# One wide matmul for state and outputs, and the right sides moved to the front of the slot

## The reference

```
bS = einsum('bhk,bhkv->bhv', b_t, S)
S  = exp(g)[..., None] * S + a_t[..., None] * bS[:, :, None, :] + k_t[..., None] * v_t[:, :, None, :]
o  = einsum('bhk,bhkv->bhv', q_t, S)
```

## Time and profile before

| | |
|---|---|
| median of 3 runs | 2630.47 us (2616.48 to 2632.16) |
| span of the profiled execution, first to last instruction | 2622.0 us |
| PE / DVE / ACT / POOL busy | 87% / 61% / 62% / 17% |
| DMA | 338.90 MB, 129 GB/s mean, queue q1 busy 48.2% |
| granted PE clock, mean | 0.950 |

### The profile page before, as it was taken

The page is one execution under the profiler, slowest core; times in us unless marked ns, Lnnn a source line. Parts: engine busy times, 40 slices in busy tenths (PEclk is TensorE's granted clock), DMA queues, the critical chain, the costliest instruction groups (busy, mean ns, idle before and its releaser), DMA issues.

```text
span 2622.0 us, 225147 instructions
## 1 busy us (share of the span) xinstructions
PE 2288.4 (87%) x102472; PEld 1721.9 (66%) x102472; DVE 1601.7 (61%) x3940; ACT 1618.0 (62%) x3048; POOL 458.8 (17%) x555
## 2 busy tenths in 40 slices
PE   6788898999988899998999998989999988999785
PEld 2556666666666666666676666666666666766573
DVE  2456366666556676656666665666666566666533
ACT  3556466666666666656666666666666666666543
POOL 1011111111111111111111111111111111111210
PEclk7879899999999999999999999999999999999987
DMA  3244455534555554455554455555445555534541
GB/s 95 74 110 121 110 148 148 141 104 127 145 141 151 137 141 111 132 138 146 144 137 118 124 145 146 148 141 142 113 129 143 145 148 148 136 103 132 140 125 41
DMA packets 692934, 338.90 MB, mean 129 GB/s; under 512 B 551794, under 2 KB 651728, under 8 KB 692816
## 3 DMA queue, kind: packets, MB, share of 16 engines
q1 hardware_dynamic: 692816, 337.67, 48.2%
HBM read 35.57 MB, written 16.78 MB: 20 GB/s over the span
## 4 chain that ended last, share of the span: by engine, by line
PE 86%; issue 10%; DVE 2%; ACT 1%; DMA 1%; SPq 0%; ACTq 0%; DVEq 0%
PE bank L570 14%; PE bank L733 13%; PE bank L712 11%; PE bank L704 8%; PE bank L724 7%; PE bank L716 5%; PE bank L593 5%; PE bank L683 5%; PE bank L622 5%; PE bank L643 3%; PE bank L577 3%; PE bank L694 2%; PE bank L602 2%; PE bank L587 2%; PE bank L584 2%
## 5 line engine op out<-in xcount | busy, mean ns | idle before, releaser
L473 POOL TENSOR_TENSOR state<-moved,edge 128x512 f32<-128x512 f32 x252 | 292.3, 1160 | 1821.9 <-DVE moved L1093 1821.9
L712 PE MATMUL bank<-parts,w_now 32*32 32x64 f32 x16512 | 420.1, 223 | 4.8 <-DMA w_now<-w_row 3.6
L570 PE MATMUL bank<-x_col,w_kqv 128*128 128x512 f32 x768 | 370.6, 619 | 48.5 <-issue 47.9
L856 ACT ACTIVATE parts<-bank,cf 128x256 f32<-128x256 f32 x512 | 214.6, 470 | 319.5 <-DVE o_col L1087 310.7
L716 PE MATMUL bank<-aq_now,delta 32*32 32x16 f32 x16512 | 403.7, 179 | 9.2 <-issue 9.2
L716 PEld LDWEIGHTS bank<-aq_now,delta 32*32 32x32 f32 x16512 | 391.7, 110 | 6.7 <-issue 6.7
L712 PEld LDWEIGHTS bank<-parts,w_now 32*32 32x32 f32 x16512 | 377.2, 110 | 17.1 <-issue 5.0
L733 PE MATMUL bank<-uq_now,s_now 32*32 32x24 f32 x32768 | 362.2, 189 | 14.5 <-issue 14.4
L733 PEld LDWEIGHTS bank<-uq_now,s_now 32*32 32x32 f32 x32768 | 337.1, 107 | 24.1 <-issue 18.2
L1116 DVE COPY_PREDICATED aq<-ci,bank 128x128 f32<-128x128 int32 x256 | 77.1, 301 | 410.3 <-PE bank L704 276.7
L1087 DVE TENSOR_TENSOR o_col<-qs,bank 128x64 f32<-128x64 f32 x512 | 89.5, 216 | 388.6 <-PE bank L716 384.7
(11 more groups left out here) (99 smaller groups left out, 3814.1 us busy)
## 6 DMA issues: line engine op xcount, KB each, us to landing
s_now<-state SPq DMA_DIRECT2D x256, 256.0 KB
uq_now<-uqv SPq DMA_DIRECT2D x256, 192.0 KB
t_now<-t_t SPq DMA_DIRECT2D x256, 128.0 KB, 2.0
w_now<-w_row SPq DMA_DIRECT2D x256, 128.0 KB
uq_a<-uqv SPq DMA_DIRECT2D x64, 384.0 KB
low<-uqv SPq DMA_DIRECT2D x64, 384.0 KB
x_col<-in_xt_dram SPq DMA_DIRECT2D x32, 512.0 KB, 5.8
w_a<-w_col SPq DMA_DIRECT2D x64, 256.0 KB
```

What stands on the lines that cost most here:

```text
L473: pool.tensor_tensor(state[:, qc, :, :, :].rearrange("p m b v -> p (m b) v"), moved[m % 2][:, :, :, :].rearrange("p m b v -> p (m b) v"), ...
L570: mm = pe.matmul(ps[:, :], w_kqv[:, a, w, f * P:(f + 1) * P], x_col[:, a, :], start=a == 0, stop=a == KT - 1)
L712: pe.matmul(ds_bank[quarter(h), m, :, :].rearrange("p b v -> p (b v)"), w_now[quarter(h), m, :], parts[quarter(h), m, :, :].rearrange("p b ...
L856: act.activation(parts[:, :, b, :], p2_bank, ACT.Copy, scale=cf[:, C_TAKE + b:C_TAKE + b + 1])
```

## The change

`updates` becomes one matmul per tile and head, of 80 columns: `delta` is now the weights, and the moving side is `wa_now`, which holds the masked rows of w for sequence 0 (32 columns) and for sequence 1 (32 columns) and `aq` (16 columns). The change of the state comes out transposed. So:

- PE: `updates` is 32 matmuls of 80 columns in place of 32 of 64 and 32 of 16. A slot runs `right_sides`, `deltas`, `updates`, then the dense work. `right_sides` waits for `first_in` (the loads of `uq_now` and `s_now`) and for `qs_copied` of the slot before; `deltas` for `second_in` (`t_now` and the `aq` piece); `updates` for `w_masked`.
- SP: the load of `w_now` is gone. The order of issue in a slot stays `t_now`, `aq`, then `uq_now` and `s_now`.
- POOL: a new `mask_part` ahead of each `decay_part`, two one-input multiplications of 128x256 from `w_row` into `wa_now`. `decay_part` has a new addition state + change (128x512) ahead of the multiplication by the decay.
- DVE: L1093 is replaced by two transposes of 128x256 from PSUM into `change`.
- ACT: the two copies to `parts` are gone; the copy to `delta` stays.

```diff
+    PIECE = GB * TB
+    WIDE = GB * HD + PIECE
+    PIECES = WIDE // PIECE
...
-        w_now = sb("w_now", [P, CT, HD])
-        parts = sb("parts", [P, CT, GB, HD])
-        aq_now = sb("aq_now", [P, CT, GB * TB])
+        wa_now = sb("wa_now", [P, PIECES, CT, PIECE])
...
-        ds_bank = psum[2][:, :].rearrange("p (m b v) -> p m b v", m=CT, b=GB)
+        up_bank = wide[:, :, 0:QI * WIDE].rearrange("p f (q c) -> p f q c", c=WIDE)
+        p2_bank = wide[:, :, QI * WIDE:QI * (WIDE + HD)].rearrange("p f (q v) -> p f q v", v=HD)
...  (SP, behind p3_filled)
-                        sp.dma_start(aq_now[:, :, :],
-                                     chunk(aq[c if n >= 1 else 1 - c], m)).then_inc(aq_in.handle, 16)
-                        sp.dma_start(by_pairs(w_now[:, :, :]),
-                                     of_chunks(by_pairs(w_row[c if n >= 1 else 1 - c][:, :, :]),
-                                               m)).then_inc(w_in.handle, 16)
+                        sp.dma_start(wa_now[:, PIECES - 1, :, :],
+                                     chunk(aq[c if n >= 1 else 1 - c], m)).then_inc(second_in.handle, 16)
...  (POOL)
+            def mask_part(j, c, n):
...
+                rows = of_chunks(by_pairs(w_row[own][:, :, :]), m).rearrange("p q (f k e) -> p q f k e", f=HF, e=PIECE)
...
+                pool.wait_ge(p3_filled.handle, made)
+                for b in range(GB):
+                    dst = wa_now[:, 2 * b:2 * b + 2, :, :].rearrange("p k (q f) e -> p q f k e", f=HF)
+                    pool.tensor_scalar(dst, rows, cf[:, C_TAKE + b:C_TAKE + b + 1], None,
+                                       ALU.mult).then_inc(w_masked.handle, 1)
...  (POOL, decay_part)
+                mine = state[:, qc, :, :, :].rearrange("p m b v -> p (m b) v")
+                pool.wait_ge(s_turned.handle, s_turned.at(g, m + 1))
+                pool.tensor_tensor(mine, mine, change[m % 2][:, :, :, :].rearrange("p m b v -> p (m b) v"),
+                                   ALU.add).then_inc(s_added.handle, 1)
                 pool.wait_ge(s_added.handle, s_added.at(g, m + 1))
...
-                pool.tensor_tensor(state[:, qc, :, :, :].rearrange("p m b v -> p (m b) v"),
-                                   moved[m % 2][:, :, :, :].rearrange("p m b v -> p (m b) v"),
-                                   decay.unsqueeze(2).to_broadcast([P, CT * GB, HD]),
+                pool.tensor_tensor(mine, mine, decay.unsqueeze(2).to_broadcast([P, CT * GB, HD]),
                                    ALU.mult).then_inc(state_ready.handle, 1)
...  (PE, updates)
-                        pe.matmul(ds_bank[quarter(h), m, :, :].rearrange("p b v -> p (b v)"), w_now[quarter(h), m, :],
-                                  parts[quarter(h), m, :, :].rearrange("p b v -> p (b v)"),
-                                  start=True, stop=True)
-                    for h in range(HPH):
-                        mm = pe.matmul(o_bank[quarter(h), m, :], delta[quarter(h), m, :], aq_now[quarter(h), m, :],
-                                       start=True, stop=True)
+                        mm = pe.matmul(up_bank[quarter(h), m % HF, m // HF, :].rearrange("p (k e) -> p k e", e=PIECE),
+                                       delta[quarter(h), m, :], wa_now[quarter(h), :, m, :], start=True, stop=True)
...  (PE, slot)
-                pe.wait_ge(x_turned.handle, turn)
-                pe.wait_ge(t_in.handle, turn16)
-                pe.wait_ge(delta_ready.handle, turn)
-                pe.wait_ge(o_added.handle, turn)
-                deltas()
-
-                pe.wait_ge(set_up.handle, N_SET_UP)
-                pe.wait_ge(w_in.handle, turn16)
-                pe.wait_ge(aq_in.handle, turn16)
-                pe.wait_ge(s_added.handle, turn)
-                updates()
-
-                pe.wait_ge(set_up.handle, N_SET_UP)
-                pe.wait_ge(uq_in.handle, turn16)
-                pe.wait_ge(s_in.handle, turn16)
+                pe.wait_ge(first_in.handle, turn32)
                 pe.wait_ge(qs_copied.handle, turn)
                 right_sides()
+
+                pe.wait_ge(set_up.handle, N_SET_UP)
+                pe.wait_ge(second_in.handle, turn32)
+                deltas()
+
+                pe.wait_ge(set_up.handle, N_SET_UP)
+                pe.wait_ge(w_masked.handle, turn2)
+                updates()
...  (ACT, delta_part)
-                act.wait_ge(o_added.handle, o_added.at(j, n - 1))
-                for b in range(GB):
-                    act.activation(parts[:, :, b, :], p2_bank, ACT.Copy, scale=cf[:, C_TAKE + b:C_TAKE + b + 1])
-                act.activation(delta[:, :, :], p2_bank, ACT.Copy).then_inc(delta_ready.handle, 1)
+                act.wait_ge(s_turned.handle, s_turned.at(j, n - 1))
+                act.activation(delta[:, :, :].rearrange("p (q f) v -> p f q v", f=HF), p2_bank,
+                               ACT.Copy).then_inc(delta_ready.handle, 1)
...  (DVE, update)
-                dve.tensor_tensor(moved[m % 2][:, :, :, :], mine, ds_bank, ALU.add).then_inc(s_added.handle, 1)
+                dst = change[m % 2][:, :, :, :].rearrange("p (q f) b v -> p f q (b v)", f=HF)
+                for f in range(HF):
+                    last = dve.transpose(dst[:, f, :, :], up_bank[:, f, :, 0:GB * HD])
+                last.then_inc(s_turned.handle, 1)
```

More of the change, by code:

```diff
@@ L165, in delta_block @@
         t_now = sb("t_now", [P, CT, HD])
-        w_now = sb("w_now", [P, CT, HD])
-        parts = sb("parts", [P, CT, GB, HD])
-        aq_now = sb("aq_now", [P, CT, GB * TB])
+        wa_now = sb("wa_now", [P, PIECES, CT, PIECE])
         state = sb("state", [P, QC, CT, GB, HD])
-        moved = [sb(f"moved{c}", [P, CT, GB, HD]) for c in range(2)]
+        change = [sb(f"change{c}", [P, CT, GB, HD]) for c in range(2)]
         x_now = sb("x_now", [P, CT, HD])
@@ L196, in delta_block @@
         lora_b = y_col[0:UD, 0, D:2 * D]
-        psum = [ctx.enter_context(nc.psum_tensor(f"bank{i}", [P, BANK], F32)) for i in range(8)]
+        wide = ctx.enter_context(nc.psum_tensor("wide", [P, HF, BANK], F32))
+        single = [ctx.enter_context(nc.psum_tensor(f"bank{i}", [P, BANK], F32)) for i in range(6)]
+        psum = [single[0], wide[:, 0, :], wide[:, 1, :]] + single[1:]
         p1_bank = psum[0][:, 0:CT * GB * RQ].rearrange("p (m b r) -> p m b r", m=CT, b=GB)
-        p2_bank = psum[1][:, 0:CT * HD].rearrange("p (m v) -> p m v", m=CT)
-        o_bank = psum[1][:, CT * HD:CT * (HD + GB * TB)].rearrange("p (m r) -> p m r", m=CT)
-        ds_bank = psum[2][:, :].rearrange("p (m b v) -> p m b v", m=CT, b=GB)
+        up_bank = wide[:, :, 0:QI * WIDE].rearrange("p f (q c) -> p f q c", c=WIDE)
+        p2_bank = wide[:, :, QI * WIDE:QI * (WIDE + HD)].rearrange("p f (q v) -> p f q v", v=HD)
         a_banks = [psum[3 + i][:, 0:CT * GB * RQ].rearrange("p (m b r) -> p m b r", m=CT, b=GB) for i in range(PAIR)]
@@ L358, in stage_first @@
             def stage_first(c, n):
-                sp.dma_start(uq_now[:, :, :], of_chunks(uqv[c][:, :, 0:HF * UQ], n)).then_inc(uq_in.handle, 16)
-                sp.dma_start(s_now[:, :, :, :], state[:, n % QC, :, :, :]).then_inc(s_in.handle, 16)
+                sp.dma_start(uq_now[:, :, :], of_chunks(uqv[c][:, :, 0:HF * UQ], n)).then_inc(first_in.handle, 16)
+                sp.dma_start(s_now[:, :, :, :], state[:, n % QC, :, :, :]).then_inc(first_in.handle, 16)
             def iteration(j, c):
@@ L456, in _ @@
             pool.wait_ge(weights_in.handle, n_weights)
+            def mask_part(j, c, n):
+                if not (there(j) and not (isinstance(j, int) and j * CH + n == 0) or (there(j - 1) and n < 1)):
+                    return
+                g, m, own = (j, n - 1, c) if n >= 1 else (j - 1, CH - 1, 1 - c)
+                rows = of_chunks(by_pairs(w_row[own][:, :, :]), m).rearrange("p q (f k e) -> p q f k e", f=HF, e=PIECE)
+                if m == 0:
+                    pool.wait_ge(w_turned.handle, w_turned.at(g, 1))
+                made = held(pool, until, p3_filled.at(j, n + 1))
+                pool.wait_ge(set_up.handle, N_SET_UP)
+                pool.wait_ge(p3_filled.handle, made)
[3 more added lines that the diff above has]
+                                       ALU.mult).then_inc(w_masked.handle, 1)
             def decay_part(j, c, n):
@@ L723, in deltas @@
                     for h in range(HPH):
-                        mm = pe.matmul(p2_bank[quarter(h), m, :], t_now[quarter(h), m, :], x_now[quarter(h), m, :],
+                        mm = pe.matmul(p2_bank[quarter(h), m % HF, m // HF, :], t_now[quarter(h), m, :], x_now[quarter(h), m, :],
                                        start=True, stop=True)
```

56 lines of the change are left out of this document (28 added, 28 removed).

## The result

The changed kernel takes 2745.21 us (median of 4 runs, 2732.57 to 2755.27), the kernel before beside it 2631.31: a ratio of 1.0455 over all their runs, with a 95% interval of 1.0399 to 1.0511 (the two medians alone give 1.043). So it is 4.5% slower. Forecast were 2720 and a range of 2590 to 2790. The profiled execution is the fastest of the four, 2732.57, on a span of 2730.7.

What follows compares the result with a forecast made beforehand. PE bounds A; PE and DVE run neck and neck in B. A 41.0 + B 37.8 = 78.8 against 75.9 us, +2.9 times 31 groups = +90 on 2622, 2712; the median lies 8.5 higher: 2720, range 2590 to 2790.

Steps and rivals of the forecast that it cites:

- B: Stretch from the end of `updates` in slot 4 to slot 0's first scores: 34.6 us before, forecast 37.8.
- `updates` from 1.53 to 1.10 us: On PE, the 80-column matmuls shorten `updates` by 0.43 us per slot, with bounds of 0.35 and 0.83.
- A: Stretch from slot 0's first scores to the end of `updates` in slot 4: 41.3 us before, forecast 41.0, bound by PE.
- Loads hidden in slots 4 to 6, 0.9 us in slot 7: Later-issued `uq_now` and `s_now` hide behind the dense part by 0.6 us in slots 4 to 6; slot 7 stalls 0.9.
- U: The end of `updates` in a slot, from which load times are counted; `s` was forecast landed 3.7 us after it.
- DVE's four gaps in B go, -1.5 us: DVE's waits for PE in B (0.33, 0.23, 0.40, 0.54 us) vanish, since `right_sides` is done before DVE's update.
- Masks 0.45 each, at most 0.73: Time on POOL of each of the two new one-input products of 128x256: 0.45 us, upper end 0.73.
- Contention, 4.1 us in B: POOL's work delays DVE's two-SBUF-input instructions, 0.8 us per us: 2.2, 0.5, 0.95, 0.45 in slots 4 to 7.
- The signs: Expected in the trace: `updates` 1.1 us, POOL near 1,200 us, longer solve and L1246, B 37 to 38 us.
- Rival 3: On PE, the 80-column matmul is no shorter than both were: 2773 us; chance 0.1 together with dearer POOL work.
- rival 2: In B, half the contention, 2.05 us, making a group 76.75 us and the time 2657; chance 0.16.
- Rival 1: In DVE's solve and products in B, no contention worth naming: group 74.7 us, time 2593; chance 0.24.

Runs made afterwards that it cites:

- 5: The changed kernel with PE's order put back to deltas, updates, right sides: 2689.83 us, 1.0225 of the kernel before.
- 8: The changed kernel with masks on ACT, PE's old order and POOL's addition of state and change left out: 2579.14 us, 0.9827 of the kernel before.
- 4: The changed kernel with the loads of `uq_now` and `s_now` issued earlier, right behind `right_sides`: 2732.44 us, 1.0426 of the kernel before.
- 2: The kernel before with only PE's order changed to right sides, deltas, updates: 2810.70 us, ratio 1.0688.
- 9: The changed kernel, new order kept, with masks on ACT and without POOL's addition of state and change: 2574.67 us, 0.9802 of the kernel before.
- 10: The changed kernel without POOL's addition of state and change, masks still on POOL: 2583.45 us, 0.9845 of the kernel before.
- 3: The kernel before with PE's new order and the loads of `uq_now` and `s_now` issued first, right behind `right_sides`: 2683.81 us, ratio 1.0227.
- 1: The kernel before with four unused 128x256 instructions on POOL per slot, two one-input and two two-input: 2760.93 us, ratio 1.0517.
- 6: The changed kernel with the masks moved from POOL to ACT: 2673.26 us, 1.0177 of the kernel before.
- 11: The changed kernel with six unused 512-column matmuls per group, three before slot 0's first scores, three in slot 5: 2680.66 us, 1.0211 of the kernel before.
- 7: The changed kernel with masks on ACT and PE's order of the kernel before: 2628.32 us, 1.0009 of the kernel before.
- Experiment 12: The changed kernel with masks on ACT, PE's old order and two unused matmuls in slot 0: 2645.26 us, 1.0081 of the kernel before.

## Why the prediction was right

It was right in sign, in size (2720 against 2745) and in the mechanism (POOL's new work delays DVE, which sets B), but terms of both stretches were wrong and partly cancelled. Point by point:

- **`updates` from 1.53 to 1.10 us: right,** 1.10 in 5. That it pays when POOL gets no more work is shown by 8, with the addition left out: 1.7% at most.
- **A at 41.0 us: 39.5.** PE's busy time in A fell by 0.74 us, from 37.82 to 37.08, where +1.42 and four times -0.43 made -0.30, and its idle time fell from 3.5 to 2.4, which I had left as it was. Why was not tested.
- **Loads hidden in slots 4 to 6, 0.9 us in slot 7: right in effect, not in the steps.** `s_now` is issued 1.4 us behind `updates` (1444.18), as I had it, and takes 2.7 us to land (median), not 2.2, so it lands at U + 4.1 and not at U + 3.7. Slot 7 did not stall, because its dense part, with a wait of 1.34 us for L1275, was longer. In the whole span PE waits 39.8 us for `s_now`, in 18 waits, and taking them out (4) brings 0.3%. How near it was is shown by 2 (150.5 us, with the old load of w ahead) and by 9 and 10 (74 us, with PE less late by DVE).
- **DVE's four gaps in B go, -1.5 us: the step that failed.** DVE's idle time in B was 3.0 us and is 2.5. In the changed kernel one large gap stands where the four stood:

```profile
1462.43 0.35 DVE L1093 TENSOR_TENSOR o_col<-qs,wide 128x64 f32<-128x64 f32 x2 [1.11 <-PE wide L729]
```

  I took the gaps in front of L1087 and L1100 as DVE waiting for a late helper, and removed the wait with the move. But PE can be late because it has waited for DVE a little before: here L729 is behind the stop of 3.39 us, which was for DVE's L1227. In 3 too the gaps came back in front of L1087, and B kept its length. I expected of 2 no more than 1.5%; the order costs 59 us in the narrow form (3) and 55 in the wide (5). But 9 shows that this is no fixed price: in the wide form, with POOL's load as before, it costs nothing.
- **Transposes +0.14 per slot: about right.** 423 ns each where I took 450, and two of them 0.09 us more of DVE's busy time than the addition.
- **Masks 0.45 each, at most 0.73: wrong.** They take 0.92 at least and 1.02 in the mean. A one-input product was dearer than the two-input addition of its size (0.73). The Trainium skill (GPSIMD Engine Reference, section 4, When to use GPSIMD) puts one-input operations near line rate; these masks don't show it, and the measurement decides. That they write strided pieces of 16 elements is not the reason: the products of 1, on whole rows, have a median of 0.92 as well. Addition 1.25: 1.26 at least, 1.41 in the mean. So POOL is busy 1,366 us, not near 1,200.
- **Contention, 4.1 us in B: too small.** From the two timelines, the instructions that I had priced grew by 2.5 us in slot 4, 0.6 in slot 5, 1.3 in slot 6 and 1.0 in slot 7, 5.4 in all, where I had 2.2, 0.5, 0.95 and 0.45. 0.8 us lost per us of POOL's two-input work was sound (the decay took 0.85 of 0.98 from L1266). By the timelines the dearer masks push it out further, and the one-input L1216 (0.85) was not in my list. Shown by 1 without any of the rest, and by 6, 8, 9 and 10 by taking it away.
- **The signs: half right.** B is 39.7 us, above the 37 to 38. I had expected L1246 well above 1.59. It fell, as L1255, to a mean of 1.21, because in slot 6 it now starts before the addition; there the addition took 2.03 us instead of 1.26, and the loss fell on the next, L1250 (now L1259), which went from 1.23 to 2.05.
- **Where PE would wait: right for the scores,** which have 76.4 us of waits, 2.5 per group, where they had 17.9. I had also named `right_sides` of slot 0 (the `issue` wait of L746 rose from 14.4 to 49.6 us, over all slots). Not named were the dense parts whose banks come free with DVE's additions to `h_row` and `x_row`, the largest together, 136 us.
- **Rival 3 (80 columns no shorter than both were)** falls with the 1.10 us, **rival 2 (half the contention)** with the 5.4.
- **Rival 1 (no contention, 2593):** its condition does not hold. The kernels with at most the masks on POOL came to 2575, 2579 and 2583, near its figure, but they leave out the addition, so they don't measure it.
- **The sum:** 41.0 + 37.8 = 78.8 was forecast, 39.5 + 39.7 = 79.2 measured. A was forecast 1.5 us too long and B 1.9 too short. That the total is near is luck, and no proof of the steps. Over all groups the mean rose by 3.0 us where 2.9 was forecast; 17 us of the 109 lie outside the 31 groups.
- **Not foreseen: the clock.** The mean granted clock fell from 0.950 to 0.919. With the two levels 1.00 and 0.50 that is (1 - 0.919)/0.5 = 16% of the span at 1.2 GHz, where it was 10%. That the stops of PE cost more than their own length is shown by 11.

**What stays open.** How the 162 us of the addition (10) split between DVE's own loss and the clock: DVE has 141 us less to do there and the clock is 0.952, both at once. Why the new order costs 59 us in the narrow form with POOL's load as before (3), and nothing in the wide form (9). And what makes the clock fall where PE hardly stands: 7, 8 and the kernel before have falls too, at clocks of 0.932, 0.933 and 0.950, and their order is not that of their times. Experiment 12 says that filling one wait isn't enough.

## What to carry to other kernels

Before work goes to a POOL with much free time, lay it over DVE's timeline. In these traces it was nearly free beside DVE instructions that read PSUM. A two-input instruction of POOL stopped those of DVE with two SBUF inputs for about as long as it ran, and one with one input too; a one-input product of POOL did so far less, but it pushed the others out. A busy share says nothing of this. Where two engines wait for one another by turns, don't credit a reordering with the gaps it closes on one; follow what that engine's partner waits for. And price costs on such a stretch together, for here the masks and the order cost next to nothing in the wide form without the addition (9 us and nothing), and 72 and 55 on top of it.

## What the runs showed of the hardware

- A two-input instruction of DVE on SBUF that started while a two-input one of POOL's ran ended about 0.13 us behind it: 128x112 in 1.19 us where it took 0.28 before. The one-input L1216 was stopped too (1.53 us instead of 0.68). A one-input product of POOL took nothing from L1266 in 63 overlaps. PSUM readers were not delayed (679 ns with three times POOL's load).
- A one-input product of 128x256 on POOL took 0.92 us, in strided pieces or on whole rows, and a two-input addition of that size 0.73.
- The clock fell behind stops of PE that were short. The stop of slot 5 as a whole, in the columns of the stretches above:

```profile
1451.00:1455.00 4.00, 0.61 (x3) 0.14 (x2) 3.83 (x13) 1.11 (x3) 2.35 (x4) 1.00 0.44 131
1455.00:1459.50 4.50, 4.50 (x25) 1.51 (x29) 4.47 (x6) 2.59 (x5) 1.04 (x1) 0.62 0.00 0
```

  PE is busy 0.61 of 4 us at a clock of 1.00, and is then fully busy at a mean of 0.62: the clock is low when the stop is over.
- Six discarded matmuls per group gained 65 us of 2745, and two at another place lost 17. Here such fillers measure what the clock costs and are no cure: neither kernel with them was faster than the one before.
